# Convolution with fewer weight matrices: shifted copies by DMA, empty columns zeroed by VectorE

## The reference

```python
x = x + conv(group_norm(x), bias, up_filter, dn_filter)   # L0
t = t + attention(layer_norm(t), Wq, Wk, Wv)              # causal, 1024 tokens per image
t = t + experts(layer_norm(t), gate, weight1, weight2)    # top 8 tokens per expert, 16 experts
```

```python
x = x + bias
x = repeat(repeat(x, 2, axis=2), 2, axis=3)    # twice the size
x = conv_same(x, up_filter)                    # 12 x 12 taps
x = leaky_relu(x, 0.2) * sqrt(2)
x = conv_same(x, dn_filter)                    # 12 x 12 taps
x = x[:, :, ::2, ::2]                          # back to 32 x 32
```

## Time and profile before

| | |
|---|---|
| median of 3 runs | 368.98 us |
| the profiled execution: its own time | 368.35 us |
| its span, first to last instruction | 366.5 us |
| TensorE busy (mean granted clock) | 327.2 us, 89% of the span (0.948) |
| VectorE, ScalarE, GpSimd busy | 260.1, 183.9 and 128.8 us |
| convolution matmuls (L892) | 480 of `up` and 480 of `down`, 56.4 and 55.1 us busy |
| chain that ended last | TensorE 77%, VectorE 10%, DMA 5% |

### The profile page before, as it was taken

How to read it: one execution, slowest core, us unless ns; L and a number is a source line. 1 busy time by engine, 2 the same in 40 slices (tenths; PEclk the granted TensorE clock), 3 DMA queues, 4 the chain that set the end, 5 groups by cost and what they waited for, 6 DMA issues and landing times.

```text
span 366.5 us, 8381 instructions
## 1 busy us (share of the span) xinstructions
PE 327.2 (89%) x3362; PEld 249.3 (68%) x3362; DVE 260.1 (71%) x523; ACT 183.9 (50%) x251; POOL 128.8 (35%) x96
## 2 busy tenths in 40 slices
PE   2289998799999999999899999999996986979985
PEld 1168886587777878786678787777774544546774
DVE  2679779957757877869686876776988786454632
ACT  1043355446557574757663755576564547440500
POOL 6134535332444337554211557312235400351000
PEclk9999999999999999999999999999999899995655
DMA  4910100001011010101000101011021100100122
GB/s 125 204 36 3 26 19 16 16 16 31 16 18 26 5 32 2 31 4 32 15 16 2 31 15 17 17 16 26 7 58 32 31 2 18 28 2 29 57 75 69
DMA packets 35906, 11.16 MB, mean 30 GB/s; under 512 B 24431, under 2 KB 35741, under 8 KB 35869
## 3 DMA queue, kind: packets, MB, share of 16 engines
q1 hardware_dynamic: 33152, 9.98, 11.3%
q10 hardware_dynamic: 2717, 0.66, 1.2%
HBM read 5.72 MB, written 4.21 MB: 27 GB/s over the span
## 4 chain that ended last, share of the span: by engine, by line
PE 77%; DVE 10%; DMA 5%; issue 3%; ACT 2%; POOL 1%; ACTq 1%; SPq 0%; DVEq 0%; POOLq 0%
PE psB L892 14%; PE psA L892 13%; PE psB L1025 9%; PE psB L1005 8%; PE psA L990 7%; PE psA L1070 4%; PE psA L882 3%; PE psA L1048 3%; PE psB L1039 3%; DVE negmax L757 2%; PE psA L993 2%; PE psA L983 2%; PE psA L1032 2%; PE psB L1008 2%; PE psB L977 2%
## 5 line engine op out<-in xcount | busy, mean ns | idle before, releaser
L757 DVE TENSOR_REDUCE negmax<-psA 128x1 f32<-128x512 f32 (+7 forms) x128 | 90.5, 751 | 32.2 <-PE psA L993 31.6
L587 ACT ACTIVATE Pp<-psB 128x1024 f32<-128x1024 f32 (+1 forms) x80 | 73.6, 937 | 35.3 <-PE psB L1008 30.7
L892 PE MATMUL psB<-xin,UU 128*128 128x224 f16 (+1 forms) x480 | 56.4, 277 | 0.1
L892 PE MATMUL psA<-y,DD 128*128 128x224 f16 (+1 forms) x480 | 55.1, 273 | 0.0
L990 PE MATMUL psA<-zK,yQ 128*128 128x512 f16 (+1 forms) x192 | 47.8, 332 | 6.0 <-DVE uT L775 2.4
L892 PEld LDWEIGHTS psB<-xin,UU 128*128 128x128 f16 x480 | 47.0, 99 | 7.9 <-DVE xin L698 0.5
L1005 PE MATMUL psB<-yQ,zK 128*128 128x512 f16 (+1 forms) x192 | 47.3, 330 | 3.7 <-DMA yQ<-rows 2.4
L892 PEld LDWEIGHTS psA<-y,DD 128*128 128x128 f16 x480 | 46.7, 98 | 5.5
L477 POOL TENSOR_TENSOR zrstd<-zrstd,power 128x8 f32<-128x8 f32 x16 | 27.2, 1698 | 53.9 <-DVE zrstd L735 53.9
L557 ACT ACTIVATE y<-psB 128x1024 f16<-128x1024 f32 x16 | 16.4, 1023 | 44.8 <-PE psB L892 44.8
L499 POOL TENSOR_TENSOR y<-y 128x1024 f16<-128x1024 f32 x16 | 34.1, 2132 | 9.8 <-ACT y L560 9.8
(11 more groups left out here) (158 smaller groups left out, 504.5 us busy)
## 6 DMA issues: line engine op xcount, KB each, us to landing
x_all<-in_x_dram SPq DMA_DIRECT2D x4, 512.0 KB, 3.9
normalised_tokens<-z SPq DMA_DIRECT2D x16, 128.0 KB, 1.8
zV<-normalised_tokens SPq DMA_DIRECT2D x64, 32.0 KB, 2.1
out_dram<-x_all SPq DMA_DIRECT2D x8, 256.0 KB, 2.3
yQ<-rows SPq DMA_DIRECT2D x32, 2.0 KB
Pp<-filter_tables ACTq DMA_DIRECT2D x4, 121.9 KB, 3.7
w_halves<-y SPq DMA_DIRECT2D x12, 32.0 KB, 1.8
cst<-shape_constants SPq DMA_DIRECT2D x1, 326.5 KB, 4.3
```

The source lines that it names most:

```text
L587: nc.scalar.activation(Pp[:, n % 2, UOFF[e[2]]:UOFF[e[2]] + N], slot(e)[:, 0:N], ACT.Exp).then_inc(b_drained, 1)
L757: ins = nc.vector.tensor_reduce(negmax[:, n % 2, m - 1:m], s[:, at:at + P * m], X, ALU.max, negate=True)
L892: ins = nc.tensor.matmul(within(out_cols, -shift), m, within(v, shift), start=i == 0, stop=i == len(matrices) - 1)
```

## The change

Two matrices that stand a shift of two apart (k = -1 and 1) use different rows of the filter: one has its rows in the lower two blocks of partitions empty, the other in the upper two. The change puts the two into one matrix and puts the data for both into one tile: partitions 0 to 63 hold the columns moved by one to the left, partitions 64 to 127 those moved by one to the right. That saves one matrix of `up` for part 1 and one for part 2 (8 instead of 10), and one matrix of `down` (9 instead of 10). Images 0 and 1 (`PLAIN_UP = 2`) keep ten in `up`.

- New tiles `mixed` (for `xin`, two groups) and `y_mixed` (for `y`, two images).
- SyncE issues two copies each, inside the core's memory, in the events `image_low` and `y_low`, and two more (`filter_wrap`) that put the filter rows into their second place in `UU`. VectorE does that for `DD` with one copy more.
- A copied row runs over the edge of the picture in one column of eight. VectorE sets these columns to zero: new events `edges` (before `up` of images 2, 4, 8 and 12) and `y_edges` (before `down` of every image), two memsets each.
- TensorE waits for `edges_zero` before `up` of images 2, 4, 8 and 12, and for `y_edges_zero` inside every `down`, ahead of its last three matmuls, which have 256 columns.

```diff
@@ STEP
-        group(6, "logit_exp"), batch(5, "up"), once(13, "w1", 0), ...
+        group(6, "logit_exp"), *[once(GB * g - 5, "edges", g) for g in range(1, G)], once(PLAIN_UP - 5, "edges", 0), batch(5, "up"), ...
-        batch(4, "down"), once(-2, "image", 1), once(-3, "small", 2),
+        batch(4, "y_edges"), batch(4, "down"), once(-2, "image", 1), once(-3, "small", 2),
@@ tiles
+        mixed = sb("mixed", [P, 2, 2, SLOT], F16)
+        y_mixed = sb("y_mixed", [P, 2, 2, BC], F16)
+        def filter_wrap(r):
+            q, n = slice(C * r, C * r + C), r - 1
+            return (UU[q, :, SPAN - n:SPAN, :, :].rearrange("p i m q t -> p i (m q t)"),
+                    U_parts[q, :, 0:n, :, :].rearrange("p i m q t -> p i (m q t)"))
@@ SyncE
+            for r in (R - 2, R - 1):
+                place_to, place_from = filter_wrap(r)
+                sp.dma_start(place_to, place_from).then_inc(UU_wrapped, 16)
+                elif name == "image_low":
+                    if g >= 2:
+                        sp.wait_ge(b_filled, BU["up", GB * (g - 1) - 1] + 1)
+                    sp.wait_ge(xin_ready, 2 * g + 2)
+                    first = BC * PLAIN_UP if g == 0 else 0
+                    v = xin[:, g % 2, :].bitcast(F16).rearrange("p (j n) -> p j n", j=2)
+                    sp.dma_start(mixed[0:2 * C, g % 2, :, first:SLOT - 1], v[0:2 * C, :, first + 1:SLOT]).then_inc(mixed_loaded[g % 2], 16)
+                    sp.dma_start(mixed[2 * C:P, g % 2, :, first + 1:SLOT], v[2 * C:P, :, first:SLOT - 1]).then_inc(mixed_loaded[g % 2], 16)
+                elif name == "y_low":
+                    sp.wait_ge(y_ready, g + 1)
+                    if g >= 2:
+                        sp.wait_ge(a_filled, A["down", g - 2] + 1)
+                    v = y[:, g % 2, :].bitcast(F16).rearrange("p (j t n) -> p j t n", j=2, t=R)
+                    sp.dma_start(y_mixed[0:2 * C, g % 2, :, 0:BC - 1], v[0:2 * C, :, 2, 1:BC]).then_inc(y_mixed_loaded[g % 2], 16)
+                    sp.dma_start(y_mixed[2 * C:P, g % 2, :, 1:BC], v[2 * C:P, :, 1, 0:BC - 1]).then_inc(y_mixed_loaded[g % 2], 16)
@@ VectorE
+                elif name == "edges":
+                    dve.wait_ge(mixed_loaded[n % 2], 32 * (n // 2 + 1))
+                    first = BC * PLAIN_UP if n == 0 else 0
+                    nc.vector.memset(mixed[0:2 * C, n % 2, :, first + JW - 1:SLOT:JW], 0.0)
+                    nc.vector.memset(mixed[2 * C:P, n % 2, :, first:SLOT:JW], 0.0).then_inc(edges_zero, 1)
+                    nc.vector.tensor_copy(DD[2 * C:P, :, SPAN - 1, 0, :], D_parts[2 * C:P, :, 0, :])
+                elif name == "y_edges":
+                    dve.wait_ge(y_mixed_loaded[n % 2], 32 * (n // 2 + 1))
+                    nc.vector.memset(y_mixed[0:2 * C, n % 2, :, JW - 1:BC:JW], 0.0)
+                    nc.vector.memset(y_mixed[2 * C:P, n % 2, :, 0:BC:JW], 0.0).then_inc(y_edges_zero, 1)
@@ TensorE, up
+                    if n == PLAIN_UP or n > 0 and n % GB == 0:
+                        pe.wait_ge(UU_wrapped, 16 * 2)
+                        pe.wait_ge(edges_zero, n // GB + 1)
+                    both = [mixed[:, n // GB % 2, j, of] for j in range(2)]
...
+                        if 1 <= t <= 2 and n >= PLAIN_UP:
+                            outer = [(UU[:, i, R - t + NS - 1, :, :], both[j], 0) for i, j in ((0, 0), (0, 1), (1, 0))]
+                        else:
+                            outer = [(UU[0:rows, i, R * k - t + NS - 1, :, :], parts[j][0:rows], k)
+                                     for k, rows in ((-1, P), (1, 2 * C if 1 <= t <= 2 else P)) if 0 <= R * k - t + NS - 1 < SPAN
+                                     for i, j in ((0, 0), (0, 1), (1, 0))]
+                                       [(UU[:, i, NS - 1 - t, :, :], parts[j], 0) for i, j in ((0, 0), (0, 1), (1, 0))] + outer)
@@ TensorE, down
+                    convolve(s[:, 0:BC], [... 24 products ... if 0 < R * k + t + 3 < SPAN - 1 ...], last=False)
+                    pe.wait_ge(y_edges_zero, n + 1)
+                    ins = convolve(s[:, 0:BC], [(DD[:, i, SPAN - 1, :, :], y_mixed[:, n % 2, j, :], 0) for i, j in ((0, 0), (0, 1), (1, 0))], first=False)
```

More of the change, by code:

```diff
@@ L41 @@
 HOMES = 4
+PLAIN_UP = 2
 SLOT = 1024
@@ L135 @@
         batch(0, "prob", 1), group(4, "proj", 1), batch(1, "score", 0), group(6, "select"),
-        group(6, "logit_exp"), batch(5, "up"), once(13, "w1", 0), group(7, "wT"), batch(0, "prob", 2),
+        group(6, "logit_exp"), *[once(GB * g - 5, "edges", g) for g in range(1, G)], once(PLAIN_UP - 5, "edges", 0), batch(5, "up"), once(13, "w1", 0), group(7, "wT"), batch(0, "prob", 2),
         once(2, "image", 2), once(6, "image", 3), once(1, "gn_var", 2), group(3, "mean", 0), once(18, "mean", 3, 1),
@@ L341, in hybrid_kernel @@
         U_ready = sem("U_ready")
-        UU_ready, UU_copied = sem("UU_ready"), sem("UU_copied")
+        UU_ready, UU_copied, UU_wrapped = sem("UU_ready"), sem("UU_copied"), sem("UU_wrapped")
+        mixed_loaded, edges_zero = [sem(f"mixed_loaded{i}") for i in range(2)], sem("edges_zero")
         sums_ready, U_split = sem("sums_ready"), sem("U_split")
@@ L348, in hybrid_kernel @@
         y_ready = sem("y_ready")
+        y_mixed_loaded, y_edges_zero = [sem(f"y_mixed_loaded{i}") for i in range(2)], sem("y_edges_zero")
         z_squared = sem("z_squared")
@@ L581, in _ @@
                         act.wait_ge(UU_ready, 16 * 2)
+                        act.wait_ge(UU_wrapped, 16 * 2)
                         act.wait_ge(UU_copied, 2)
@@ L887, in within, with convolve @@
                 return v.rearrange("p (h j) -> p h j", j=JW)[:, :, max(0, shift):JW + min(0, shift)]
-            def convolve(out_cols, matrices):
+            def convolve(out_cols, matrices, first=True, last=True):
                 for i, (m, v, shift) in enumerate(sorted(matrices, key=lambda a: a[2] != 0)):
-                    ins = nc.tensor.matmul(within(out_cols, -shift), m, within(v, shift), start=i == 0, stop=i == len(matrices) - 1)
+                    ins = nc.tensor.matmul(within(out_cols, -shift), m, within(v, shift), start=first and i == 0, stop=last and i == len(matrices) - 1)
                 return ins
@@ L952, in _ @@
                         pe.wait_ge(UU_copied, 2)
-                    parts = [v[:, BC * (n % GB):BC * (n % GB) + BC] for v in img[n // GB % 2]]
-                    for t in range(R):
+                    if n == PLAIN_UP or n > 0 and n % GB == 0:
+                        pe.wait_ge(UU_wrapped, 16 * 2)
+                        pe.wait_ge(edges_zero, n // GB + 1)
+                    of = slice(BC * (n % GB), BC * (n % GB) + BC)
+                    parts = [v[:, of] for v in img[n // GB % 2]]
+                    both = [mixed[:, n // GB % 2, j, of] for j in range(2)]
+                    for t in range(R):
+                        if 1 <= t <= 2 and n >= PLAIN_UP:
[4 more added lines that the diff above has]
+                                     for i, j in ((0, 0), (0, 1), (1, 0))]
                         ins = convolve(s[:, BC * t:BC * t + BC],
-                                       [(UU[:, i, R * k - t + NS - 1, :, :], parts[j], k) for k in (-1, 0, 1) if 0 <= R * k - t + NS - 1 < SPAN
-                                        for i, j in ((0, 0), (0, 1), (1, 0))])
+                                       [(UU[:, i, NS - 1 - t, :, :], parts[j], 0) for i, j in ((0, 0), (0, 1), (1, 0))] + outer)
                 elif name == "down":
@@ L962, in _ @@
                         pe.wait_ge(a_drained, A["dnT", 0] + 1)
-                    ins = convolve(s[:, 0:BC], [(DD[:, i, R * k + t + 3, :, :], y_parts[n % 2][j][:, BC * t:BC * t + BC], k) for k in (-1, 0, 1)
-                                                for t in range(R) if 0 <= R * k + t + 3 < SPAN for i, j in ((0, 0), (0, 1), (1, 0))])
+                    convolve(s[:, 0:BC], [(DD[:, i, R * k + t + 3, :, :], y_parts[n % 2][j][:, BC * t:BC * t + BC], k) for k in (-1, 0, 1)
+                                          for t in range(R) if 0 < R * k + t + 3 < SPAN - 1 for i, j in ((0, 0), (0, 1), (1, 0))], last=False)
+                    pe.wait_ge(y_edges_zero, n + 1)
+                    ins = convolve(s[:, 0:BC], [(DD[:, i, SPAN - 1, :, :], y_mixed[:, n % 2, j, :], 0) for i, j in ((0, 0), (0, 1), (1, 0))], first=False)
                 elif name == "tok":
```

## The result

The changed kernel takes 407.56 us (median of 4 runs, 406.99 to 412.05) against 368.52 us for the kernel before on the same chip: ratio 1.109, 95% interval 1.100 to 1.117. It is slower by 39 us. Forecast were 381.5 us and a range up to 390: the direction was right, the size three times too small. The profiled execution of the changed kernel took 406.99 us, its span 405.1 us, against 368.35 and 366.5 before: 38.6 us to explain.

The account below looks back on a forecast made before the run. TensorE was taken to bound the main loop. `up` +1.4, `down` +10.9 and clock less slack +0.8 made +13.1 on the profiled 368.35: 381.5 us, range 371 to 390.

Parts of the forecast that it names:

- 24 and 27 matmuls at 109 ns: TensorE's merged `up` and every `down`: 9.18 and 5.25 us saved, together 14.43 us if nothing waits.
- The place on VectorE: Inside each `down`, TensorE waits for memsets behind VectorE's earlier work: `down` as a whole +10.9 us instead of -5.25.
- Rival 1: Waits in `down` are hidden, so it keeps its -5.25 and only `up` (+1.4) remains: 364.5 us; chance 0.09.
- rival 3: VectorE and GpSimd set the time until 100 us, so only what lies behind counts: +2.3, 371 us; chance 0.08.
- Rival 2: Memsets held until GpSimd's subtraction ends, 2.26 us later in images 4, 9, 10, 13, 14: +11.3, 393 us; chance 0.07.
- I take 0.35 us for the pair of 64 elements: Price of VectorE's memset pairs before TensorE's waits in `down` and `up`: 0.35, 0.4 or 0.6 us by size.
- Image 12: its copies are issued a step earlier, nothing: Before `up` of image 12, copies are issued a step earlier, so its wait was put at nothing.
- The step on the clock, +1.7: Half clock after the stall before image 4 loses 1.7 us (0 to 3.4, as it may follow image 8 too).
- The landing, 2.9 us from the issue: Copies before `up` of images 4 and 8, 262 KB each, land 2.9 us after issue (2.3 to 3.9).
- Images 8 and 12 as plain steps: `down` of these images counted among seven plain steps, -0.1 to +0.1 for image 10, about -0.2 in all.
- Slack: Small earlier waits that a later TensorE no longer meets: 0.9 us taken off (0 to 4).
- Plain images 0 and 1: `up` of images 0 and 1 keeps 30 matmuls; no saving or added cost was counted.

Follow-up runs that it names:

- experiment 4: Changed kernel without `edges` and `y_edges`, TensorE waiting for the copies themselves, tiles zeroed once by GpSimd: 374.28 us, ratio 1.016.
- experiment 3: Changed kernel with each memset cut to one element at its same place, tiles zeroed once at the front by GpSimd: 390.47 us, ratio 1.060.
- Experiment 7: Changed kernel with useless matmuls filling TensorE's stalls before `up` of images 4, 8 and 12: 404.05 us, ratio 1.096.
- experiment 1: Change in `down` alone, every `up` keeping 30 matmuls (`PLAIN_UP = 16`, no `mixed`, its copies or `edges`): 391.92 us, ratio 1.064 to the kernel before.
- experiment 13: Both convolutions on data padded to nine places a row, zeros set once by VectorE at the front: 364.04 us, ratio 0.989 to the kernel before.

## Why the prediction was wrong

**What held.** 24 and 27 matmuls at 109 ns: ten ups are 0.66 us shorter, as reckoned, and so is every `down` by 0.33 where nothing waits (experiment 4). The place on VectorE: idle of 1.56 to 1.81 us inside `down` of images 9, 11, 13 and 15 (1.4 to 1.7 forecast; +1.40 to +1.66 net, 1.1 to 1.3 forecast), +1.19 for image 0 (1.35 forecast). Rival 1 (waits hidden) and rival 3 (the front absorbs) are out: of the 18.8 us that the downs cost 1.25 are given back, and at `down` of image 5 TensorE is already 18.4 us late. Rival 2 is out for memsets. The direction is no luck, then; the size is what failed, by the steps below.

**The step "I take 0.35 us for the pair of 64 elements (0.15 to 0.8), 0.4 for the pair of 128 (image 2), 0.6 for the pair of 256 (0.35 to 1.6)".** This was the largest error and sits in every `down` and in the four ups. The rows that I priced by were arithmetic, most of it on float32 side by side (1024 in 1.28 us); the memsets write 2-byte elements with a stride, and 4.4 ns an element is mostly idle time that stands in no row. From the end of what is ahead to TensorE's start the traces show 0.73 us where I had 0.45, 1.36 in image 2 where I had 0.5 (`z_rstd` ends at 40.82, start 42.18), and 2.61 in image 4 where I had 0.7. In the downs that is 0.28 each, some 4 us; in the ups of images 2, 4 and 8 some 5 us. The upper bound for 64 elements (0.8) was not reached, but that for 256 (1.6) was passed. Experiment 3 shows the price apart from the place: with one element in each memset the downs cost +10.6 in all instead of +18.8, and ups 2, 4, 8 and 12 start 1.8, 5.7, 4.3 and 2.1 us later instead of 2.9, 8.0, 6.5 and 3.8.

**The step "Image 12: its copies are issued a step earlier, nothing".** For `down` I listed what stands ahead of the memsets on VectorE, for `up` of image 12 I looked at the copies alone. They landed in time, but `edges` stands behind `yQ` and `score`:

```profile
220.15 1.23 DVE L797 TENSOR_REDUCE negmax<-psA 128x1 f32<-128x1024 f32 x1
222.23 0.27 DVE L733 MEMSET mixed<- 64x256 f16 x1 [0.86 <-issue]
223.46 0.27 DVE L734 MEMSET mixed<- 64x256 f16 x1 [0.96 <-issue]
...
223.88 2.08 PE L932 MATMUL psB<-xin,UU 128*128 128x256 f16 x9 [3.84 <-DVE mixed L734]
```

3.82 us, and the clock behind it. With memsets of one element (experiment 3) 2.1 of it stay: that is the place alone.

**The step on the clock, +1.7.** I priced one stall by the row of half clock for 3.41 us. Five stalls brought it. Three times the whole `up` of 24 matmuls ran at half speed: 1.69 + 0.66 = 2.35 us each, and 1.38 in image 2, 8.4 in all. The fifth is the wait inside `down` of image 3, and 1.5 us behind it were lost, as the part on slack shows. Experiment 7 shows the 2.35 directly: three ups at full clock once the stalls are filled.

**The landing, 2.9 us from the issue.** It took 4.05 in image 4, above the upper bound of 3.9 that 512 KB had shown. About 1 us in images 4 and 8 each.

**Images 8 and 12 as plain steps.** They cost 1.02 us each instead of nothing. In these steps VectorE's `split_z` now meets GpSimd's work on `u` (image 8):

```profile
171.66 1.04 POOL L540 TENSOR_TENSOR u<-t_all,nmean 128x512 f32<-128x512 f32 x1
171.78 1.20 DVE L784 TENSOR_TENSOR z<-centred,zrstd 128x248 f32<-128x248 f32 x1
```

L784 takes 0.42 in most steps; here it ends after L540, 0.8 later, and the memsets behind it too. In experiment 1, where the steps lie otherwise, both images cost 0.18.

**Slack.** I let the idle 1.30 and 0.76 after images 3 and 5 pay for part of the wait and took 0.9 off, 2.96 in all. Image 3 cost 3.10 and gave back 0.22, image 5 cost 3.39 and gave back 1.03. The idle 1.30 behind image 3 is gone as I reckoned, but the clock took its place. Here is the same work of TensorE behind `down` of image 3, in the trace after and in that of before (columns as in rows 1):

```profile
86.27:90.01 3.74, 3.74 (x26) 2.84 (x24) 2.22 (x4) 1.02 (x1) 0.00 (x0) 0.58 0.25 71
67.96:70.18 2.22, 2.22 (x25) 1.84 (x26) 2.19 (x6) 1.02 (x1) 0.00 (x0) 1.00 0.01 1
```

At a granted clock of 0.58 it takes 1.5 us more. Experiment 1 has the half clock in the same place (74.50 to 77.91) without a stall before `up` of image 4, so it belongs to the wait in `down` of image 3 and not to that stall, as the expectation of experiment 1 had it. But for the clock 1.25 + 1.5 = 2.8 us would have been given back: the slack itself was about right.

**Plain images 0 and 1.** I took them as unchanged. With half the rows in six of their matmuls they cost 0.4 each.

Together: 4 (downs) and 5 (ups) for the memsets, 3.8 for image 12, 8.2 for the clock (8.4 + 1.5 less the 1.7 forecast), 2 for landings, 1.6 for images 8 and 12, 0.2 for the slack, 0.8 for the plain images make 25.6 us, in rounded terms, where 25.5 lie between forecast and trace. The split between memset and landing within images 4 and 8 rests on one row each.

## What to carry to other kernels

In this kernel a few matmuls saved on the bounding engine were worth their 0.1 us each only where the operand that replaces them was ready without that engine waiting; here the releaser was VectorE, behind all its older work, and some 53 us were lost where 14.4 were saved. List for every new wait what stands ahead of its releaser on its own engine, in each step in which it occurs, and price the stall with the half clock behind it. Where data must be padded with zeros, lay it out so that the zeros are set once (experiment 13), and set them on an engine that is idle then.

## What the runs showed of the hardware that was not expected

- A strided 2-byte memset on VectorE costs 4.4 ns an element (282 ns for 64, 2.24 us for 512), of which its row shows 112 ns and 0.48 us; the rest appears as idle "issue" ahead of it. A float32 memset at a stride starts each 112 ns for 64, side by side each 66 to 76.
- A strided float16 copy of 64 elements takes 0.31 us alone and 2.07 us when it starts inside a GpSimd `tensor_tensor`; a memset in the same place is not held. A VectorE copy at the front took 5.45 us instead of 0.43 and ended with GpSimd's memsets, in four kernels that had them there; with them on VectorE it took 0.51.
- A matmul on 256 columns with a gap after every eighth takes 122 to 123 ns, side by side 109; 224 columns, seven of each eight, take 109 to 110, and 111 with the gap.
- Six of 30 matmuls on 64 rows instead of 128 lengthen an `up` from 3.45 to 3.86 us.
- Copies inside SBUF in pieces of 14 bytes: 28 KB land in 7.2 us (median) and take up to 2.5 us to issue; 64 KB in pieces of 510 bytes landed in 2.1.
